# Four pairs of batches routed inside attention, at three batches a pair, in place of three at four batches a pair

## What is computed

```python
x = x + 0.5 * ffn(layernorm(x))
x = x + attention(layernorm(x))          # 16 heads of 8
x = x + 0.5 * ffn(layernorm(x))

def ffn(h):                              # 8 experts, 2 of them for each token
    scores = softmax(h @ gate_w.T)
    w, i = top_k(scores, 2); w = 2.5 * w / (w.sum() + 1e-20)
    y = sum over the two chosen experts of w * (silu(h @ w_gate) * (h @ w_up)) @ w_down   # F = 176
    return y + (silu(h @ sw_gate) * (h @ sw_up)) @ sw_down                                 # shared, F = 352
```

## Time and profile before

| What | Value |
|---|---|
| median of 3 runs | 1761.1 us (1755.4 to 1765.99) |
| the profiled execution | 1749.63 us |
| its span, first to last instruction | 1747.9 us, so 1.7 us lie around it |
| mean granted TensorE clock | 0.923 |
| busy share of the span | PE 81%, DVE 78%, ACT 63%, POOL 54% |

### The profile page before, as it was taken

The page is one execution under the profiler, slowest core; times in us unless marked ns, Lnnn a source line. Parts: engine busy times, 40 slices in busy tenths (PEclk is TensorE's granted clock), DMA queues, the critical chain, the costliest instruction groups (busy, mean ns, idle before and its releaser), DMA issues. The chain is left out here.

```text
span 1747.9 us, 26225 instructions
## 1 busy us (share of the span) xinstructions
PE 1422.1 (81%) x8158; PEld 796.4 (46%) x8158; DVE 1360.5 (78%) x2729; ACT 1102.3 (63%) x1688; POOL 947.2 (54%) x1040
## 2 busy tenths in 40 slices
PE   5788869996278999889988999888887795888846
PEld 3566647774123333333333333333325573666624
DVE  6777848885368888888888888888847784998938
ACT  6554447774047777777777777777667553766623
POOL 3676734223545554567744775544312673677765
PEclk9888989998569999999999999999998897999978
DMA  6411258784111100111111011111001114676727
GB/s 238 160 47 41 89 169 253 258 260 156 62 53 50 51 32 28 52 58 60 58 54 45 25 61 53 50 43 53 14 2 50 44 51 144 223 240 223 235 79 284
DMA packets 76459, 181.26 MB, mean 104 GB/s; under 512 B 19776, under 2 KB 21408, under 8 KB 76000
## 3 DMA queue, kind: packets, MB, share of 16 engines
q1 hardware_dynamic: 53408, 141.74, 24.4%
q0 software_dynamic: 21376, 37.03, 6.5%
q10 hardware_dynamic: 1536, 0.80, 0.2%
HBM read 105.03 MB, written 55.30 MB: 92 GB/s over the span
## 5 line engine op out<-in xcount | busy, mean ns | idle before, releaser
L2063 DVE TENSOR_REDUCE attn_neg_max<-attn_p_score 128x2 f32<-128x1024 f32 x512 | 623.4, 1222 | 122.7 <-PE attn_p_score L1718 118.2
L1869 ACT ACTIVATE attn_exps<-attn_p_score 128x1024 f32<-128x1024 f32 x512 | 521.7, 1025 | 218.2 <-PE attn_p_score L1704 215.7
L1718 PE MATMUL attn_p_score<-k_pack,q_pack 32*128 32x512 f32 x1024 | 262.2, 511 | 47.6 <-ACT attn_exps L1869 23.7
L1735 PE MATMUL attn_p_o<-attn_exps,values 128*32 128x512 f32 x2048 | 278.7, 616 | 8.6 <-ACT attn_o_raw L1875 3.3
L748 POOL DMA_INDIRECT rows<-send_rows,queue_slots x208 | 214.0, 1029 | 105.9 <-issue 60.3
L1704 PE MATMUL attn_p_score<-q_pack,k_pack 32*128 32x512 f32 x1024 | 255.7, 505 | 2.4 <-DVE attn_neg_max L2063 2.4
L1704 PEld LDWEIGHTS attn_p_score<-q_pack,k_pack 32*128 32x128 f32 x1024 | 95.2, 185 | 267.5 <-issue 236.0
L1362 POOL DMA_INDIRECT results<-own_y,own_to_row x156 | 155.9, 999 | 70.3 <-issue 44.2
L333 POOL DMA_INDIRECT attn_both<-results,queue_found_at x128 | 126.8, 991 | 44.1 <-issue 34.2
L1969 POOL DMA_DIRECT2D q_pack<-attn_max_rows x128 | 78.7, 617 | 124.5 <-ACT attn_max_rows L1863 120.1
L1718 PEld LDWEIGHTS attn_p_score<-k_pack,q_pack 32*128 32x128 f32 x1024 | 96.6, 187 | 97.7 <-ACT attn_exps L1869 72.9
(11 more groups left out here) (391 smaller groups left out, 3244.4 us busy)
## 6 DMA issues: line engine op xcount, KB each, us to landing
own_own<-own_weights SPq DMA_DIRECT2D x78, 640.0 KB, 4.4
own_rows<-rows SPq DMA_DIRECT2D x78, 264.0 KB, 3.3
results<-own_y SPq DMA_DIRECT2D x39, 256.0 KB, 4.7
q_pack<-attn_q_high SPq DMA_DIRECT2D x32, 256.0 KB
k_pack<-attn_k_high SPq DMA_DIRECT2D x32, 256.0 KB
sum_both<-results SPq DMA_DIRECT2D x16, 512.0 KB, 6.6
own_weights<-weights_pack SPq DMA_DIRECT2D x1, 5120.0 KB, 16.6
rows<-in_pad SPq DMA_DIRECT2D x16, 264.0 KB, 3.8
```

Source lines behind the costliest of these rows:

```text
L1718: last = nc.tensor.matmul(score_bank("max", b, n)[:, j % 2, :], pack["q"][b.par][rows, g, t * P:(t + 1) * P], pack["k"][b.par][rows, g, :] ...
L1735: last = nc.tensor.matmul(p_o[h * COLS:(h + 1) * COLS, :], values[b.par][:, t, g * QUAD + h, :], exps[(2 * u + h // 2) % len(exps)][:, h % ...
L1869: nc.scalar.activation(exps[n % len(exps)][:], score_bank("exp", b, n)[:], ACT.Exp, scale=inv_sqrt)\
L2063: V.tensor_reduce(neg_max[g % 2][:, j:j + 2, t], score_bank("max", b, n)[:], AX.X, ALU.max, negate=True).then_inc(max_read, 1)
```

## The change

Attention sends four pairs (0 to 3) with a new one every three batches. Send2 routes the four pairs 4 to 7; its order becomes (0, 4, 5, 6, 7, 1, 2, 3), so the kept pairs become 2 and 3. Nothing else is edited: ROUTED falls from 5 to 4 through NSENT.

```diff
-NSENT = 3
+NSENT = 4
 LATE = 2
-SPACED = 4
+SPACED = 3
@@ class Kept:
-    PAIRS = (1, 2)
+    PAIRS = (2, 3)
```

## The result

Over 7 runs each, the median went from 1757.5 to 1746.6 us: ratio 0.9934, 95% interval 0.9908 to 0.9959. A second comparison on another occasion had 23 runs of before, median 1757.6, and 12 of after, median 1747.2: ratio 0.9945 (0.9928 to 0.9961). So the change is faster by about 0.6%, some 10 us. I had forecast 1757 (4.2 us faster), with 1750 to 1766 as the range.

The account below looks back on a forecast made before the run. Extra PE work between batches was taken to bound attention, and POOL's scatters, with ACT, DVE and PE waiting behind them, send2. Attention's +1.4 and send2's -5.6 gave -4.2 us: 1761.1 to 1757, range 1750 to 1766.

Parts of the forecast that it names:

- The base: Whole kernel: the median before, 1761.1 us, stands 11.5 us above the profiled execution, and that difference is carried over.
- Attention, the closer spacing: Attention, batches 4, 7 and 10: steps 3 and 0 meet on DVE, +0.6 us in three, between 0 and 3.0.
- Rival B: Attention: steps 3 and 0 fill DVE, maxima come late, PE falls to the low clock; 1765 us, chance 0.11.
- Attention, the fourth pair: Attention: one more long interval with the late turn and logits, +0.8 us; the pair's other work is hidden.
- The clock in attention: Attention: batch 11 took 1.77 us more at granted clock 0.94; no clock falls there were put in the sum.
- Send2, the scatters of place 3 begin earlier: Send2: with place 5 no longer routed, these scatters begin 3.3 us earlier, between 1.7 and 4.0.
- The release for place 7: Send2, iteration 5: ACT's wait for the scatters of place 4 ends at 1438.5 instead of 1441.85.
- The block table leaves iteration 5: Send2: moving the table to iteration 4 removes a DVE stall, gaining 2.3 us, between 0 and 2.9.
- rival C: Send2: the gain does not come, place 3's slots hang on PE and ACT, another stall follows; 1762.5 us, chance 0.11.
- Rival D: Send2: PE falls to the low clock in both waits, neither fall covered; 1760.4 us, chance 0.10.
- Shared expert and scatters end together: End of send2 before: DVE's last instruction is over at 1463.34, the last scatter would land at 1463.1.
- Rival A: Send2: POOL bounds it throughout, so one pair's 16 scatters, 21.3 us, leave its end; 1741 us, chance 0.08.

Follow-up runs that it names:

- again: The kernel after, unchanged, measured and profiled once more: median 1747.2 us, ratio 0.9945 to the kernel before.
- table late: The kernel after with the count and block table put back into iteration 5 of send2: median 1748.0 us, ratio 0.9943.

## Why the prediction was wrong, step by step

*The base:* I added my -4.2 us to 1761.1, the median of three runs. All seven runs of before have 1757.5. So 3.6 of the 10.3 us between 1757 and 1746.6 are the base, and 6.7 the change.

*Attention, the closer spacing:* right at its lower bound. DVE was busy 45.15 us in batch 4 where I had 45.2, and the intervals behind the three meetings were 50.36, 50.37 and 50.43. I had put 0.6 us there; it is 0.1 or less. Rival B fell.

*Attention, the fourth pair:* the size was right (51.2 against 50.4), the cause half wrong. I laid it to the late turn and the logits; without seven of the logits the whole 0.85 is gone, with the turns still there.

*The clock in attention:* I had left the one fall of the earlier trace rows out of the sum, as if it came by chance. In all profiles every fall within batches 1 to 14 stands in a batch with step 2, and begins 1.7 to 3.5 us behind the start of its logits. The first profile of before had one of three, the second all three, the two of after three of four. The stretch took 708.8, 716.3 and 711.2 us in the three profiles with three pairs and 714.6, 714.8 and 714.5 in those with four (after, again, table late). So the change costs 2.5 us there by these means, and the difference of the first two profiles (5.8) overstated it. It is not clear of the noise: the three profiles with three pairs differ by 7.5 us among themselves. Attention's last batch, behind this stretch, took 52.5, 56.4 and 52.3 us with three pairs and 52.3 to 52.4 with four, so the whole of attention differs by +1.2. That is near my +1.4 by luck: the falls that I had left out stand against one slow last batch of before.

*Send2, the scatters of place 3 begin earlier:* right. Counted from the end of attention's last DVE instruction (1313.41 and 1317.19), they began at 85.01 before and at 81.37 after, 3.6 us earlier; I had 3.3. The hole at place 3 went from 3.09 to 0.74 us.

*The release for place 7:* 2.3 us earlier (128.44 to 126.14), not 3.3. The last scatter of place 4 was issued 4.3 us earlier, but ACT went on 4.38 us behind it, not 2.34. That is a part of the step I had left out: with the block table SP's eight pad transfers also moved forward. They were issued from 1429.4 to 1439.4, and the DMA engines' busy share from 1434 to 1444 was 0.63, where before had 0.17. The eight scatters issued from 1430.2 on took 3.5 to 4.5 us to land, the ten before them 2.3 us by their median. With the table late, and so the pads, the last nine of place 4 took 2.4 us by their median, and the release came 2.43 us behind the last issue. In the second profile of after the nine took 3.9 us by their median, but the last one of them 2.6. So the pads slow the scatters; how much of the release they cost differs from run to run.

*The block table leaves iteration 5:* wrong, 0.1 us instead of 2.3 (21.49 to 21.38 from the release to DVE's end). The 2.9 us of stall that I read between silu and product lay in a stretch of 6.8 us in which PE worked at its low clock, from 1446.45 on. In after DVE waits 3.50 us for PE's up product in the same iteration. For this one term rival C was right: the stall gave place to another. Rival D's falls came as well. PE's timeline in iteration 5 of after,

```profile
1446.83 0.51 PE L557 MATMUL send_p_y<-send_hid_high,down_high 128*128 128x512 f32 x1 [3.67 <-DVE send_hid_low L795]
1449.05 1.11 PE L583 MATMUL send_p_y<-ident,send_yt 128*128 128x128 f32 x4 [1.25 <-ACT send_yt L663]
```

has four turns in 1.11 us, against 0.66 at the full clock. A fall followed the idle stretch in iteration 4 too (1423.8 to 1430.7). That one was covered by the wait for place 4, as I had it; the one in iteration 5 was there before the change as well, so neither shows as a loss.

*"Shared expert and scatters end together":* **this is the step that failed.** I took the stage to end with the later of 1463.34 (DVE) and 1463.1 (the last landing) and compared the two by their last instruction. What opened the next stage was POOL's drain, which was over 6.6 us behind POOL's last scatter, or 5.0 us behind DVE's end. One pair fewer took POOL from there, so the opening fell from 5.24 to 0.28 us. In three profiles with three pairs it was 5.2, 6.5 and 5.3, in three with four pairs 0.3 each. I had priced the lighter end of POOL at nothing.

Put together, send2 with its opening took 155.2, 159.3 and 155.8 us with three pairs and 147.8, 147.4 and 147.4 with four: 9.2 us less by the means, of which 5.4 are the opening and 3.9 send2 itself (I had 5.6 for send2 alone; without the second profile of before, whose send2 ran at a mean clock of 0.84, it is 3.0). With attention's +1.2 that is -8.0. What lies behind the opening of own2 took 0.8 less and what lies ahead of batch 1 took 0.3 more, which makes the 8.5 us between the mean spans, 1753.9 and 1745.3. The medians are 10.4 to 10.9 us apart. Three profiles a side are too few to say more about the last 2 us.

Rival A, a full scatter period (-21.3 us in send2), did not come: DVE's end stayed 21.4 us behind ACT's release for place 7, as it was before (21.5), so the shared expert's chain behind that release does bound send2.

## What to carry to other kernels

At the end of a stage look at every engine's queue, not at its last instruction: a POOL that worked to the end of send2 kept the next stage shut for another 5.7 to 6.8 us, and one that worked to the end of send1 for 3.7, so work taken off its end can be worth that much more. An operation that others wait for should not stand behind a batch of scatters in the same queue: one root moved four scatters forward was worth 3 us in each round, 14 in send1. And before differences of a few us are summed from one profile, take a second one of the same kernel: here the two differed by 15.8 us.

## What was not expected of the hardware

PE's granted clock fell in a busy stretch. No idle time of PE above 0.5 us stands near batch 3 of the second profile of before, only 16 matmul records of 8 columns in 2.10 us; the batch took 4.1 us more than in the first profile. Thirteen profiles have it there and nowhere else between batches 1 and 14; the fourteenth, without seven eighths of these matmuls, has no fall. And the next stage opened 5.7 us behind POOL's last memset and 6.8 us behind its last scatter in send2, but 3.7 us behind its last scatter in send1.
